# Gated long convolution on one Trainium2 core: the far-pair products of the queries on GpSimd, ScalarE's high halves and TensorE's y_4 in another order

## The reference

```python
kv = jnp.einsum('bhil,bhjl->bijhl', k_, v_)          # k_ = v_ = context, 64 heads h of 8 channels
kv_f = jnp.fft.rfft(kv, n=2 * L)
kernel_f = jnp.fft.rfft(ssm_kernel, n=2 * L)
y = jnp.fft.irfft(kv_f * kernel_f, n=2 * L)[..., :L]
out = y + kv * D[None, None, None, :, None]
out = jnp.einsum('bijhl,bhil->bjhl', out, q_)        # q_ = layernorm(x)
x = x + tanh(g_xattn) * out
x = x + tanh(g_ffn) * moe(layernorm(x))              # 7 routed experts, top 2, and a shared one
```

## Time and profile before

| | |
|---|---|
| median of 3 runs | 4268.14 us (4264.76 to 4273.23) |
| profiled execution, its own time | 4265.89 us |
| its span in the trace | 4264.1 us |
| TensorE busy in the span | 97% |
| VectorE busy | 61% |
| ScalarE busy | 44% |
| GpSimd busy | 23% |
| mean granted TensorE clock | 0.99 |

### The profile page before, as it was taken

The page is one execution under the profiler, slowest core; times in us unless marked ns, Lnnn a source line. Parts: engine busy times, 40 slices in busy tenths (PEclk is TensorE's granted clock), DMA queues, the critical chain, the costliest instruction groups (busy, mean ns, idle before and its releaser), DMA issues.

```text
span 4264.1 us, 71266 instructions
## 1 busy us (share of the span) xinstructions
PE 4125.0 (97%) x25930; PEld 3759.3 (88%) x25930; DVE 2600.3 (61%) x2980; ACT 1890.9 (44%) x2451; POOL 987.7 (23%) x1200
## 2 busy tenths in 40 slices
PE   6999999999999999996899999999999999999998
PEld 6999999999999999995788788888898888988986
DVE  5999999999999999995343432222223323323331
ACT  6787777777778777772111111111112212212120
POOL 1333233332333323230000024540011111211111
PEclk9999999999999999997999999999999999999999
DMA  7888988889888898887223234233433433443332
GB/s 168 223 217 212 222 212 220 217 213 221 213 218 218 212 222 212 220 211 126 87 74 104 87 92 129 75 113 97 119 95 97 114 76 97 95 99 99 83 93 47
DMA packets 280375, 634.14 MB, mean 149 GB/s; under 512 B 45840, under 2 KB 111866, under 8 KB 280246
## 3 DMA queue, kind: packets, MB, share of 16 engines
q1 hardware_dynamic: 218582, 413.89, 33.9%
q0 software_dynamic: 61664, 218.41, 26.6%
HBM read 311.03 MB, written 170.16 MB: 113 GB/s over the span
## 4 chain that ended last, share of the span: by engine, by line
PE 49%; DMA 2%; DVE 1%; issue 1%; ACT 0%; SPq 0%; POOL 0%; DVEq 0%; POOLq 0%; ACTq 0%
PE moe_ps L1654 11%; PE moe_ps L1655 11%; PE moe_ps L1656 11%; PE moe_ps L1672 5%; PE moe_ps L1674 5%; PE moe_ps L1673 5%; PE moe_psT L1643 1%; DMA out<-moe_y,moe_add_i 1%; DMA moe_y<-out 1%; DVE moe_zl L1552 1%; DMA out<-moe_y 0%; ACT moe_zh L1324 0%; DVE moe_hid L1565 0%; DVE moe_y L1579 0%; DMA moe_zin<-zT_d 0%
## 5 line engine op out<-in xcount | busy, mean ns | idle before, releaser
L1654 PE MATMUL moe_ps<-moe_zh,moe_w1h 128*128 128x512 f32 (+2 forms) x2368 | 861.1, 364 | 36.6 <-DVE moe_zl L1552 22.1
L1655 PE MATMUL moe_ps<-moe_zl,moe_w1h 128*128 128x512 f32 (+2 forms) x2368 | 859.0, 363 | 0.0
L1656 PE MATMUL moe_ps<-moe_zh,moe_w1l 128*128 128x512 f32 (+2 forms) x2368 | 856.6, 362 | 0.0
L693 PE MATMUL att_psY<-att_kv_hi,att_tz_hi 128*128 128x288 f32 x2560 | 775.4, 303 | 51.4 <-DMA att_kv_lo<-att_kv 43.6
L695 PE MATMUL att_psY<-att_kv_hi,att_tz_lo 128*128 128x288 f32 x2560 | 755.7, 295 | 0.0
L694 PE MATMUL att_psY<-att_kv_lo,att_tz_hi 128*128 128x288 f32 x2560 | 755.5, 295 | 0.0
L1565 DVE TENSOR_TENSOR moe_hid<-moe_ps,moe_act_s 128x512 f32<-128x512 f32 (+2 forms) x148 | 91.6, 619 | 890.1 <-PE moe_ps L1656 871.4
L693 PEld LDWEIGHTS att_psY<-att_kv_hi,att_tz_hi 128*128 128x128 f32 x2560 | 481.6, 188 | 68.4 <-issue 57.8
L1654 PEld LDWEIGHTS moe_ps<-moe_zh,moe_w1h 128*128 128x128 f32 x2368 | 446.0, 188 | 89.2 <-issue 38.1
L1656 PEld LDWEIGHTS moe_ps<-moe_zh,moe_w1l 128*128 128x128 f32 x2368 | 447.7, 189 | 51.3
L1655 PEld LDWEIGHTS moe_ps<-moe_zl,moe_w1h 128*128 128x128 f32 x2368 | 446.5, 189 | 50.6 <-issue 0.2
(11 more groups left out here) (188 smaller groups left out, 7926.9 us busy)
## 6 DMA issues: line engine op xcount, KB each, us to landing
att_kv_lo<-att_kv POOLq DMA_DIRECT2D x128, 1152.0 KB, 12.3
att_kT<-in_cT SPq DMA_DIRECT2D x64, 512.0 KB, 11.6
att_xn<-in_x SPq DMA_DIRECT2D x64, 512.0 KB, 5.8
out<-att_x SPq DMA_DIRECT2D x64, 512.0 KB, 4.0
z_d<-att_z SPq DMA_DIRECT2D x64, 512.0 KB, 9.0
zT_d<-att_zT SPq DMA_DIRECT2D x64, 512.0 KB, 5.3
moe_zin<-zT_d SPq DMA_DIRECT2D x64, 512.0 KB, 4.9
moe_y<-out SPq DMA_DIRECT2D x128, 256.0 KB, 4.3
```

Of the source, the lines that this page charges most:

```text
L693: nc.tensor.matmul(acc, w_hi[:, cols], x_hi, start=start, stop=False, skip_group_check=True)
L1654: nc.tensor.matmul(acc, w1h[:, c, cols], zh[:, c, 0:w], start=(c == 0), stop=False)
L1655: nc.tensor.matmul(acc, w1h[:, c, cols], zl[:, c, 0:w], start=False, stop=False)
L1656: last = nc.tensor.matmul(acc, w1l[:, c, cols], zh[:, c, 0:w], start=False, stop=(c == C - 1))
```

## The change

On VectorE `multiply` keeps the two near products; the two far ones go to a new GpSimd function `multiply_far`, with a semaphore `far_done`. `add_up` waits for both. GpSimd runs `multiply_far(h - 1, 1 - u, 1)` first in step h and `multiply_far(h, u, 0)` last. `conv_out` and `queries`, which overwrite `y` and `qx`, wait for `far_done` beside `multiplied`. On ScalarE `high(h + 1, 1 - u, 1)` moves ahead of `conv_out(h, 5)`, and `minus_high(h + 1, 1 - u, 1)` to right behind `minus_v(h, 1, ...)`; `keys` and `keys_on` stand behind it. On TensorE the terms of tile 4 that use half 0 of the keys come first, for both halves of the batch, and only the last term waits for half 1 of the keys.

```diff
@@ blocks(a)
         if a < G + 2:
-            return near + [("S", a + 2 - c, c) for c in (2, 3)]
+            return [("S", a + 2 - c, c) for c in (2, 3)] + near
@@ GpSimd
+            def multiply_far(h, u, half):
+
+                pool.wait_ge(y_set, NT * h + G * (half + 1))
+                pool.wait_ge(q_set, 4 * h + 2 * (half + 1))
+                wait(pool, added, 3 * (2 * h + half))
+                far = y[half][:, :, :, RUN:PAIRS].rearrange("p t b i -> p (t b) i")
+                nc.gpsimd.tensor_tensor(place(RUN, [HD + 1, HD // 2]), far,
+                                        runs(qx[u], half, HD // 2, [1, HD // 2]), ALU.mult)
+                nc.gpsimd.tensor_tensor(place(HD * HD - HD // 2, [1, HD // 2]), far,
+                                        runs(qx[u], half, 0, [1, HD // 2]), ALU.mult).then_inc(far_done, 1)
+
             def step(h, u, ahead, back, back2):
+                if back:
+                    multiply_far(h - 1, 1 - u, 1)
                 roots(0, h)
                 if ahead:
                     add_low(h + 1, 1 - u, 0)
@@
                 if ahead:
                     add_low(h + 1, 1 - u, 1)
+                multiply_far(h, u, 0)
 
             steady(pool, step)
+            multiply_far(H - 1, 1, 1)
             roots(1, H - 1)
@@ ScalarE, conv_out and queries
                     wait(act, multiplied, 2 * (h - 1) + n // G + 1)
+                    wait(act, far_done, 2 * (h - 1) + n // G + 1)
...
                 wait(act, multiplied, 2 * (h - 2) + half + 1)
+                wait(act, far_done, 2 * (h - 2) + half + 1)
@@ ScalarE, step
                 queries(h, u, 1)
-                if more:
-                    keys(h + 2)
+                if ahead:
+                    high(h + 1, 1 - u, 1)
                 conv_out(h, 5)
                 minus_v(h, 1, 0)
                 minus_v(h, 1, 1)
+                if ahead:
+                    minus_high(h + 1, 1 - u, 1)
+                if more:
+                    keys(h + 2)
+                conv_out(h, 6)
                 if more:
                     keys_on(h + 2)
-                if ahead:
-                    high(h + 1, 1 - u, 1)
-                conv_out(h, 6)
-                if ahead:
-                    minus_high(h + 1, 1 - u, 1)
                 if back:
                     normal_x1(h - 1)
@@ VectorE, multiply
                 nc.vector.tensor_tensor(place(RUN + 1, [HD + 1, D1], [1, HD]), near[:, :, 1:D1 + 1, :],
-                                        runs(qx[u], half, 0, [0, D1], [1, HD]), ALU.mult)
-                nc.vector.tensor_tensor(place(RUN, [HD + 1, HD // 2]), far,
-                                        runs(qx[u], half, HD // 2, [1, HD // 2]), ALU.mult)
-                nc.vector.tensor_tensor(place(HD * HD - HD // 2, [1, HD // 2]), far,
-                                        runs(qx[u], half, 0, [1, HD // 2]), ALU.mult).then_inc(multiplied, 1)
+                                        runs(qx[u], half, 0, [0, D1], [1, HD]), ALU.mult).then_inc(multiplied, 1)
@@ VectorE, add_up
                 dve.wait_ge(multiplied, 2 * h + half + 1)
+                dve.wait_ge(far_done, 2 * h + half + 1)
@@ TensorE, conv
-                if n == G:
-                    pe.wait_ge(hi_set, 2 * h + 2)
-                    pe.wait_ge(lo_in[1], 16 * h + 16)
...
-                parts = [terms[:2], terms[2:]] if n == NT - 1 else [terms]
+                parts = [terms[:2], terms[2:]] if n in (G, NT - 1) else [terms]
...
+                            if n == G and kind == "T":
+                                pe.wait_ge(hi_set, 2 * h + 2)
+                                pe.wait_ge(lo_in[1], 16 * h + 16)
```

More of the change, by code:

```diff
@@ L217, in gated_conv @@
         q_turned, q_set = m.sem("q_turned"), m.sem("q_set")
-        multiplied, added = m.sem("multiplied"), m.sem("added")
+        multiplied, far_done, added = m.sem("multiplied"), m.sem("far_done"), m.sem("added")
         o_turned = m.sem("o_turned")
@@ L233, in keys_of, with place @@
             return slice((1 - half) * G, (2 - half) * G)
+        def place(first, *dims):
+            a = prod[:, :, :]
+            return bass.AP(a.tensor, a.offset + first, [a.ap[0], [HD * HD, M], *dims])
         def runs(t, half, offset, *dims):
@@ L589, in multiply @@
                 near = ys[:, :, 0:RUN].rearrange("p m (d i) -> p m d i", i=HD)
[L590 to L594, removed]
                 nc.vector.tensor_tensor(place(0, [HD, D1 + 1], [1, HD]), near,
```

## The result

The changed kernel takes 4478.65 us, median of 4 runs (4473.08 to 4484.58), against 4268.28 us for the kernel before (also 4 runs, 4264.76 to 4273.23): ratio 1.049, 95% interval 1.047 to 1.051. It is slower by 210 us. The forecast was 4446 us, with a range of 4350 to 4530.

A forecast was written before the change was run, and what follows sets the result against it. VectorE was taken to bound the heads' stage by a hair over TensorE. Half 0's +3.0 and half 1's -0.1 made +2.9 us a step, over 61 steps +177 us: 4446 us forecast, range 4350 to 4530.

The forecast's parts named there:

- The pacer: Heads' stage: VectorE paces by a hair at 29.70 us a step, TensorE 0.3 us a step behind.
- What leaves VectorE: Far products leaving VectorE: 0.82 us in half 0 and 0.92 us in half 1, 1.74 us a step.
- The wait of half 0: VectorE's additions wait for half 0's far products, last in GpSimd's step: +3.0 us a step, net of the 0.82 saved.
- The hold of half 1: Half 1's far products on GpSimd hold back VectorE's L578 and pairs: 0.85 us a step, between 0 and 1.7.
- Rival 1: Half 1's products hold VectorE off in full, 1.7 us instead of 0.85: 52 us more, 4498; chance 0.30.
- ScalarE's order: high ahead of conv_out delays TensorE about 1 us, hidden by VectorE's wait; without it GpSimd's chain is about 1.2 us longer.
- The number of steps: Heads' stage: 61 steps pay, the first two and the last excepted, giving +177 us.
- Rivals 2 to 4: GpSimd: a far product takes 1.2 us or more, chance 0.12; GpSimd gets through first, 0.07; DMA doesn't hold it, 0.03.

The follow-up runs named there:

- both_free: Changed kernel with half 0's far products ahead of the residual's roots and each half's only after VectorE's pairs: 4252.47 us against 4274.41 for the kernel before, ratio 0.9948.
- old_orders: Changed kernel with ScalarE's and TensorE's orders as in the kernel before, far products still on GpSimd: 4555.69 us, ratio 1.066.
- free_old_orders: Far products placed on GpSimd as in both_free, with ScalarE's and TensorE's orders of the kernel before: 4245.24 us, ratio 0.9953.
- ahead: Changed kernel with half 0's far products moved ahead of the residual's roots on GpSimd: 4283.42 us against 4274.41 for the kernel before, ratio 1.0022.
- half1_free: Changed kernel, but half 1's far products also wait until VectorE's pairs are made: 4411.31 us, ratio 1.032.

## Why the prediction held, and where its sizes were off

- **The pacer** was read rightly. VectorE at 29.70 us a step with no gaps paced, TensorE 0.3 to 0.4 us behind: both_free took the work off VectorE and the step went to 29.27, where 29.4 had been said.
- **What leaves VectorE.** 0.82 in half 0 was right. In half 1 0.92 was said and 0.80 left: from the first near product to `add_up` it is 3.98 us now and was 4.78 (L596 at 1115.68 to L609 at 1120.46). `add_up` waits for VectorE's own last product in any case, and that 0.1 us moved to the near one. The row of before, and the two of now:

```profile
1115.68 2.28 DVE L596 TENSOR_TENSOR att_prod<-att_y,att_qx 128x2048 f32<-128x2048 f32 x1
```

```profile
1100.26 2.27 DVE L612 TENSOR_TENSOR att_prod<-att_y,att_qx 128x2048 f32<-128x2048 f32 x1
...
1104.24 2.29 DVE L622 TENSOR_TENSOR att_prod<-att_prod 128x2048 f32<-128x2048 f32 x1
```

- **The wait of half 0**, the term that decided: +3.0 said, +2.93 found. Every link of it is in GpSimd's timeline. The gap is 3.66 us for about 3.8. That the total is so close is in part luck: single sizes were off and cancelled, the end of the roots 0.14 us behind VectorE's `differences` for 0.05, the lag of the DMA 0.66 for 0.6, a product 0.75 us alone for 0.85.
- **The hold of half 1**: 0.85 said, as the middle of 0 and 1.7; 1.14 found, 0.57 for each product. This is the step of the sum that was mis-sized: with the 0.80 above, half 1 costs 0.34 us a step where -0.1 was said. The Trainium skill (SBUF — State Buffer, "Who interferes with whom") calls the ports that the two engines share an exclusive lock; it says so for a whole instruction where it speaks of VectorE's 2-port modes, and of an instruction with two SBUF inputs only that it contends with a GpSimd instruction that reads SBUF. The traces agree in kind: VectorE operations with two SBUF inputs were held, while the residual, with one operand in PSUM, took 0.73 us beside a product (0.74 before) and the two statistics 1.29 (1.28 before). In size VectorE lost 0.57 us of the product's 0.75, so not quite a whole instruction. Rival 1 would have had 0.75 at this duration, 1.5 for both; 1.14 lies between it and the forecast's middle, which would have been 0.75. By the total alone rival 1 (4498) was nearer to 4478.65 than the forecast (4446): the total does not decide between them, the rows do.
- **ScalarE's order** was put at nothing while VectorE waits, and needed by the chain at 1.2 us; old_orders has 1.25. As a change alone it costs 8 us, which the prediction left at "would show in part"; with the products in VectorE's free stretches nothing of it shows (free_old_orders).
- **The number of steps.** 61 were counted, all 64 pay. With 3.24 us for 2.9 and 64.5 for 61 steps, 177 us became 209; these two are the whole difference to the forecast of 4446.
- **Rivals 2 to 4** did not come about: a product takes 0.75 us; GpSimd was second at the port in the changed kernel, and where it was first, in ahead and both_free, its chain was no shorter for it (last section); and the DMA holds GpSimd, since L376 is entered at 1119.37, during the DMA, but ends only 0.81 us after the DMA's end at 1119.81.

## What to carry to other kernels

Before work goes to an idle engine, write down what is queued ahead of it there and who needs the result: GpSimd was idle for two thirds of the heads' stage, and its result still came 3.66 us late, nine microseconds after the queue ahead of it had started, because the work stood behind operations that themselves waited for the engine it was to relieve. Where GpSimd and VectorE work side by side, let a semaphore hold GpSimd until VectorE is in operations with at most one SBUF input; here that wait alone took the loss from 4.9% to 3.2% (half1_free), and with the better place in the queue from a loss of 0.2% (ahead) to a gain of 0.5% (both_free). And look at the second engine in line before hoping for much: TensorE stood 0.4 us behind VectorE, so 1.6 us a step taken off VectorE gave no more than that.

## What the runs showed of the hardware that was not expected

GpSimd sometimes does come first. In ahead and in both_free the first root operation takes 0.19 us beside L612 (2.35 in the changed kernel). GpSimd's timeline in both_free:

```profile
1112.78 0.19 POOL L352 TENSOR_TENSOR att_root<-att_mv,att_eps 128x1 f32<-128x1 f32 x1 [1.36 <-DVE att_mv L581]
1113.05 2.49 POOL L353 TENSOR_TENSOR att_root<-att_root,att_minus_half 128x1 f32<-128x1 f32 x1
1115.74 2.35 POOL L355 TENSOR_SCALAR att_root<-att_mv,att_root 128x1 f32<-128x1 f32 x1 [0.21 <-POOL att_root L353]
```

Winning the first did not help: the second and third were then caught for 2.49 and 2.35 us, and the three end 5.3 us after the first starts, where the changed kernel has 5.4. In both kernels the third root operation ends with VectorE's `differences`, the third two-input operation in the row (1118.09 and 1118.05 here, 1117.91 and 1117.77 there). It had started beside the second near product and did not get in at its end (1116.78), as L350 had not got in at the end of L602:

```profile
1115.03 1.75 DVE L615 TENSOR_TENSOR att_prod<-att_y,att_qx 128x1536 f32<-128x1536 f32 x1
1116.70 1.35 DVE L593 TENSOR_TENSOR att_diff<-att_kv 128x1152 f32<-128x1152 f32 x1
```

So the count is not one VectorE operation for each GpSimd operation: what was won at the first was lost again at the third. Why the start a hundredth of a microsecond ahead (L613 starts at 1112.79) falls the other way round in these two kernels was not tried.
